# A graph network block on one core: the mixer's last multiply and add go from VectorE to GpSimd

## What is computed

```python
xn = _layernorm(x)
x = x + gnn(xn, ...) + mix(xn[None], ...)[0]
x = x + ffn(_layernorm(x), ...)

def mix(x, Wq, Wk, Wv, Wm, W1, W2, g1, b1, g2, b2):
    Q, K, v = elu(x @ Wq) + 1, elu(x @ Wk) + 1, (x @ Wv) / L
    KV = einsum('nshd,nshv->nhdv', K, v)
    Z = 1 / (einsum('nlhd,nhd->nlh', Q, K.sum(axis=1)) + eps)
    msg = (einsum('nlhd,nhdv,nlh->nlhv', Q, KV, Z) * L).reshape(N, L, C) @ Wm
    msg = _layernorm(msg, g1, b1)
    h = relu(concatenate([x, msg], -1) @ W1) @ W2
    return x + _layernorm(h, g2, b2)        # the change is in the "* g2" and in the sum

def gnn(...):                               # per edge: a score, a softmax per target, a weighted sum
    score = sum(q_att[etype, col] * k[row]) * pri[etype] / sqrt(64)
    agg = segment_sum(softmax(score) * v_msg[etype, row], col)
    return sigmoid(skip)[node_type] * typed_matmul(agg, a_linears, node_type)
```

## Time and profile before

| | |
|---|---|
| median of 3 runs | 2380.79 us (2377.87 to 2383.92) |
| span of the profiled execution | 2514.6 us (the page gives no time around it) |
| busy in the span | PE 2034.6, DVE 1762.5, ACT 1483.8, POOL 1180.2 us |
| mean granted clock of TensorE | 0.920 |
| DMA | 587 MB, 233 GB/s over the span |

### The profile page before, as it was taken

How to read it: one execution, slowest core, us unless ns; L and a number is a source line. 1 busy time by engine, 2 the same in 40 slices (tenths; PEclk the granted TensorE clock), 3 DMA queues, 4 the chain that set the end, 5 groups by cost and what they waited for, 6 DMA issues and landing times.

```text
span 2514.6 us, 38612 instructions
## 1 busy us (share of the span) xinstructions
PE 2034.6 (81%) x10630; PEld 1506.8 (60%) x10630; DVE 1762.5 (70%) x4682; ACT 1483.8 (59%) x4969; POOL 1180.2 (47%) x1207
## 2 busy tenths in 40 slices
PE   6999998985888888888888888888888774812999
PEld 5865554544666666666666666666666553611666
DVE  8867765544788888888888888888888664626121
ACT  6755554553667677777667676777767574620222
POOL 0033334335556565656655566556656413661231
PEclk9999999987999999999999999999999887965999
DMA  5868878986788887778878888888878837840110
GB/s 186 312 239 320 326 312 286 357 344 200 234 262 245 262 254 253 251 256 253 258 238 262 258 254 266 255 256 259 264 244 245 192 79 243 278 163 31 48 58 33
DMA packets 272145, 587.07 MB, mean 233 GB/s; under 512 B 45595, under 2 KB 186145, under 8 KB 265275
## 3 DMA queue, kind: packets, MB, share of 16 engines
q0 software_dynamic: 93936, 387.70, 47.1%
q1 hardware_dynamic: 177995, 196.89, 24.2%
HBM read 407.88 MB, written 176.99 MB: 233 GB/s over the span
## 4 chain that ended last, share of the span: by engine, by line
PE 46%; DVE 18%; ACT 14%; issue 10%; another core or an unknown queue 6%; DMA 4%; DVEq 1%; SPq 1%; POOL 0%; POOLq 0%; ACTq 0%
ACT arena L1267 10%; PE bank L904 7%; PE bank L739 7%; PE bank L872 4%; PE bank L893 4%; PE bank L1061 4%; PE bank L1072 4%; PE bank L718 3%; PE bank L587 2%; DMA arena<-chunk_rel 2%; DVE arena L1873 2%; DVE arena L1883 2%; PE bank L725 1%; DVE arena L1959 1%
## 5 line engine op out<-in xcount | busy, mean ns | idle before, releaser
L2248 POOL DMA_INDIRECT arena<-table,arena x880 | 862.9, 981 | 616.6 <-PE bank L904 360.7
L1267 ACT ACTIVATE arena<-arena 128x64 f32<-128x64 f32 x3520 | 857.3, 339 | 0.0
L904 PE MATMUL bank<-arena 128*128 128x260 f32 x1760 | 494.0, 420 | 58.7 <-issue 26.4
L904 PEld LDWEIGHTS bank<-arena 128*128 128x128 f32 x1760 | 342.9, 206 | 159.8 <-issue 65.3
L1873 DVE TENSOR_TENSOR arena<-bank,arena 128x512 f32<-128x512 f32 x440 | 300.3, 684 | 112.5 <-remote 52.5
L893 PE MATMUL bank<-arena 128*128 128x256 bf16 x2640 | 339.0, 279 | 11.5 <-issue 10.2
L893 PEld LDWEIGHTS bank<-arena 128*128 128x128 bf16 x2640 | 257.5, 100 | 73.4 <-issue 14.2
L1883 DVE TENSOR_REDUCE arena<-arena 128x16 f32<-128x1024 f32 x220 | 265.7, 1208 | 11.9 <-issue 0.5
L587 PE MATMUL bank<-arena 128*128 128x128 f32 (+1 forms) x643 | 127.2, 306 | 149.9 <-issue 47.6
L739 PE MATMUL bank<-arena 64*128 64x512 f32 x832 | 211.1, 624 | 22.3 <-DVE arena L1609 11.1
L872 PE MATMUL bank<-arena 128*128 128x256 f32 (+1 forms) x800 | 198.1, 393 | 7.5 <-issue 7.5
(11 more groups left out here) (310 smaller groups left out, 2978.2 us busy)
## 6 DMA issues: line engine op xcount, KB each, us to landing
arena<-q_parts SPq DMA_DIRECT2D x440, 192.0 KB
arena<-chunk_rel SPq DMA_DIRECT2D x220, 128.0 KB
arena<-table,arena POOLq DMA_INDIRECT x880
node_rows<-arena SPq DMA_DIRECT2D x24, 512.0 KB, 7.2
xl_and_sum<-arena SPq DMA_DIRECT2D x8, 1536.0 KB
arena<-in_x SPq DMA_DIRECT2D x12, 512.0 KB, 8.6
xn<-arena SPq DMA_DIRECT2D x12, 512.0 KB, 8.6
xT<-arena SPq DMA_DIRECT2D x12, 512.0 KB, 8.1
```

The costliest lines, as they stand in the source:

```text
L904: ins = TE.matmul(bank[b][:, 0:AW], lhsT=so[p % 2][:, c % 2, j, :], rhs=ring[:, c % NR, j, EX0:EX0 + AW], start=j == 0, stop=j == HALF - 1)
L1267: ins = A.activation(seg, seg, ACT.Copy, scale=rows[:, EX0 + h:EX0 + h + 1])
L2248: G.indirect_dma_start(ring[:, i % NR, j, :], None, d_tab_rows[0:N * R, :], bass.IndirectOffsetOnAxis(ap=idxE[:, g, j, c:c + 1], axis=0)). ...
```

## The change

DVE's two operations are taken out of its mixer, and with them the half step 10 of its table. POOL gets a function `add_base(g)` with the same multiply and the same add over the same buffers. It is called ahead of the gathers of pair 14, 23, 32 and so on (every ninth, 23 times inside the loop), and for the last two groups behind the last gather. A new semaphore, `base_scaled`, orders the add behind the multiply. All that waited for `mix_base` now waits for POOL's signal.

```diff
-DVE_AT = (2, 2, 4, 7, 10)
+DVE_AT = (2, 2, 4, 7)
+BASE_AT, BASE_PERIOD = 14, 9
...
         def mix():
             until = half_steps()
-            elu, y2s, ap, nrm, bas = DVE_AT
+            elu, y2s, ap, nrm = DVE_AT
...
-                if g:
-                    yield from until(g, bas)
-                    V.wait_ge(y2_normed, g)
-                    V.wait_ge(mbase_in.sem(g - 1), mbase_in.done(g - 1))
-                    into, part = base[:, 0:n_before, :], y2[:, 0:n_before, :]
-                    t = step(V.tensor_tensor(out=part, in0=part, in1=g2row.unsqueeze(1).to_broadcast([P, n_before, C]), op=ALU.mult))
-                    V.wait_ge(dve_step, t)
-                    V.tensor_tensor(out=into, in0=into, in1=part, op=ALU.add).then_inc(mix_base, 1)
...
+        def add_base(g):
+            n = len(mtiles(g))
+            into, part = base[:, 0:n, :], y2[:, 0:n, :]
+            G.wait_ge(mixw_in, 16 * 7)
+            G.wait_ge(y2_normed, g + 1)
+            G.wait_ge(mbase_in.sem(g), mbase_in.done(g))
+            G.tensor_tensor(out=part, in0=part, in1=g2row.unsqueeze(1).to_broadcast([P, n, C]), op=ALU.mult).then_inc(base_scaled, 1)
+            G.wait_ge(base_scaled, g + 1)
+            G.tensor_tensor(out=into, in0=into, in1=part, op=ALU.add).then_inc(mix_base, 1)
+
         for p in range(NPAIR):
+            if p >= BASE_AT and (p - BASE_AT) % BASE_PERIOD == 0 and (p - BASE_AT) // BASE_PERIOD < MG:
+                add_base((p - BASE_AT) // BASE_PERIOD)
             if p >= NR // 2:
...
+
+        for g in range((NPAIR - 1 - BASE_AT) // BASE_PERIOD + 1, MG):
+            add_base(g)
```

More of the change, by code:

```diff
@@ L499, in build @@
         sem("den_ready"), sem("averaged"), sem("averaged_too"), sem("rows_used"), sem("x1_stats"), sem("wa_scaled"), sem("slots_out"))
+    base_scaled = sem("base_scaled")
     cols_ready, inv2_built = sem("cols_ready"), sem("inv2_built")
```

## The result

On one chip, against the kernel before, the changed kernel took 2387.75 us in the median (2382.05 to 2399.23, 17 runs) and the kernel before 2380.0 us (2373.3 to 2394.98, 17 runs). The ratio is 1.0035, 95% interval 1.0021 to 1.005. So it is about 8 us slower. I had forecast 2378, 2.9 us faster.

The account below looks back on a forecast made before the run. It took hand-overs between in-order queues to bound the loop, with PE and DVE about equally full. -4.2 + 0 + 0.3 + 1 = -2.9 us on 2380.8 gave 2378 us; 8-in-10 range 2358 to 2392.

Parts of the forecast that it names:

- +1: GpSimd operand reads beside DVE's operations: they may keep each other out, costing 1 us in all.
- -4.2: DVE's multiply and add leaving its mixer: of 33.8 us freed, 4.2 us come off the time.
- late gathers: POOL's gathers behind each insertion: about 2.0 us late, covered by slack before the products, 0 us.
- my band of 2373.6 to 2387.9: Whole kernel's time: within 0.3% of the forecast 2378 us, given 50%.
- The four kinds of gaps: DVE after each L1847, by group number modulo 4: gaps absorb the 1.4 us; in kind 3 PE could use 0.3.
- The chain's three visits to L1847: Chain of work that ended last: passes DVE's base multiply in 3 groups of 25, 1.4 us each, 4.2 us.
- Rival (a): DVE in the loop sets the pace: gain 9.5 us (2371), or all 33.8 us (2347); chance 32%.
- Rival (b): GpSimd keeps out DVE operations with both inputs in SBUF, 2 x 1.35 us a group: 2390 to 2401; chance 13%.
- its deciding point of 1.4 us lost a group: DVE's loss to GpSimd in the mixer groups: it decides from 1.4 us lost per group.
- My margin of 9.6 us: POOL's gathers ahead of the products: 13.9 us from issue to use, 4.3 needed, leaving 9.6 us.
- The wait for normalised rows, the store, the tail (0, 0 and +0.3 us): Base rows ready 8 to 10 us early, store signal 11 us ahead, last group's base at most +0.3 us.
- sign (a): PE in the loop: its busy share rising by over 0.5% would show that DVE sets the pace.

Follow-up runs that it names:

- e1: The kernel before, unchanged, run once more for a profile on a 2380 chip: 2379.41 us.
- e16: Changed kernel with GpSimd's two operations replaced by a one-column memset that only signals, base left out, second run on a 2380 chip: ratio 0.9992.
- the memsets: Changed kernel with GpSimd's two operations replaced by five memsets that read nothing, base left out: ratios 1.0003, 1.0019, 1.0023 on 2380 chips, 1.0343 on a 2520 chip.
- the aligned version: Changed kernel with GpSimd's two operations ahead of an odd pair, waiting for DVE's edge targets: 2379.35 us, ratio 1.0015 (2380 chip); 1.036 (2520 chip).
- e17: Changed kernel with GpSimd's two operations replaced by three one-operand copies, base left out, on a 2380 chip: ratio 1.0013.
- e4: Kernel before, DVE keeping its base work, with GpSimd doing the same two operations on rows nobody reads: 2406.15 us, ratio 1.0124.
- e12: Changed kernel with GpSimd's two operations done twice at each place, the second time on dead rows, on a 2380 chip: 2405.81 us, ratio 1.0125.
- the signal: Changed kernel with GpSimd's two operations replaced by a one-column memset that signals, base left out, on 2380 chips: ratios 1.0003 and 0.9992.
- the copies: Changed kernel with three one-operand GpSimd copies in place of its two operations, base left out, on a 2380 chip: ratio 1.0013.
- the double dose: Changed kernel with GpSimd's two operations done twice at each place: 2405.81 us, ratio 1.0125 (2380 chip); 2636.2 us, 1.0471 (2520 chip).
- e2: Changed kernel with GpSimd's two operations replaced by five memsets that read nothing, base left out, on a 2380 chip: 2374.89 us, ratio 1.0003.
- e11, e13: A follow-up run on a 2380 chip; the text does not say under this number what it changed or measured.
- e15: Changed kernel with five memsets in place of GpSimd's two operations, base left out, on a further 2380 chip: ratio 1.0023.

## Why the prediction was wrong, point by point

- **The direction.** I forecast -2.9 us and measured about +8. The step that failed is "+1", what the two engines do to each other: I put it near the floor, and it cost about 8 us. "-4.2" and "0" for late gathers were each off by some 4 us besides, which their intervals hardly tell from nothing. The time of 2387.75 us lies just inside my band of 2373.6 to 2387.9, but only because the band reached into "slower": the ratio's interval lies wholly above 1, and the mechanism behind the forecast was not what happened.
- **The worth of DVE's 33.8 us (-4.2 us).** Right in kind, a little too large. With the two operations gone and nothing in their place the ratios are 1.0003 and 0.9992, -0.6 us in the mean, with intervals of 5 and 7 us to either side, so 4.2 is not excluded by them. The four kinds of gaps behind the earlier trace rows told it rightly: the time went into DVE's wait for PE ahead of the products, 53.3 us in e1 and 79.9 in e16, 27 of the 34 us. These are the groups of the two kernels:
```profile
L1873 DVE TENSOR_TENSOR arena<-bank,arena 128x512 f32<-128x512 f32 x440 | 300.8, 685 | 59.2 <-PE bank L893 53.3 <-DMA arena<-table,arena 5.4
```
```profile
L1867 DVE TENSOR_TENSOR arena<-bank,arena 128x512 f32<-128x512 f32 x440 | 300.4, 684 | 85.9 <-PE bank L895 79.9 <-DMA arena<-table,arena 5.5
```
 In the changed kernel the same wait is 58.4 us:
```profile
L1867 DVE TENSOR_TENSOR arena<-bank,arena 128x512 f32<-128x512 f32 x440 | 300.4, 684 | 64.0 <-PE bank L895 58.4 <-DMA arena<-table,arena 4.7
```
 So of the 29 us of hold-ups some 21 went into the wait that the freed time had become, which is why they cost less than they last. The chain's three visits to L1847 are a count of places where DVE came last, not of time that would be got back. Rival (a) did not hold on 2380 chips.
- **What the two engines do to each other (+1 us).** This is the step that failed. I put it "near the floor, as most DVE operations there read a bank of PSUM or one operand". Most do, but POOL meets DVE wherever its gathers let it, and at 14 of the 23 places in the loop the multiply started about 1.36 us ahead of L1924, with make_oh between. At every one of the 14 make_oh and GpSimd's own add were held up, and at 8 of them a third operation, L1941 or L1901, too. At four places (680.8, 910.35, 1368.14 and 1828.36 us) nothing was. DVE lost 29 us over 25 groups, 1.2 us a group, close to one GpSimd operation each. The price: the changed kernel's three ratios on 2380 chips have the mean 1.0048, the memsets' three 1.0015. The difference, 0.33% or 8 us (4 to 12 by the intervals), is what the hold-ups cost, and the aligned version (1.0015), where they are gone, stands where the memsets stand. Rival (b) was the right one. Its 2 x 1.35 us a group were twice what was lost, and its 2390 to 2401 us a little too high, for I measured 2387.75, and 2391 by the mean of the ratios; its deciding point of 1.4 us lost a group was too high as well, for 1.2 us already cost. The price does not grow in proportion: 17 us of hold-ups (e17) gave a ratio of 1.0013, 29 gave 1.0048, and 42 to 44 gave 1.0124 (e4, where DVE had kept its own work) and 1.0125 (e12, where GpSimd's time had doubled too). I gave it 13%, and the sum should have taken a price between the ends.
- **How long GpSimd takes.** I said 1.35 us for each operation and measured 1.28 for the multiply and 1.27 for an add that nobody holds up; most adds were held up and took 1.81. An insertion was to take 3.3 us and takes 3.13 in the mean of 23, from its first operation to the next gather. The last group's half-width pair took 0.73 and 0.72 us against my 0.7 each.
- **Late gathers (0 us).** On 2380 chips nearly right: the memsets' mean, 0.15% or 4 us, is all that is left for GpSimd's time, and none of the three intervals lies wholly above 1.0. On 2520 chips the loss is 60 us, and 80 with memsets. My margin of 9.6 us rested on 4.3 us from issue to use at the loop's start and on one place in the loop. That place was typical of the tightest (13.9 us from issue to use; the least is 13.3 in the changed kernel), so what I costed, rows that land too late for their product, is not what the trace shows to fail; another wait, which I had no term for, grew. I never asked what the 52.5 us of products waiting for "remote" were, in the same profile.
- **The wait for normalised rows, the store, the tail (0, 0 and +0.3 us).** Right: POOL waited for ACT once, 40.3 us, before the last group, where the gathers were over. GpSimd's last add ended at 1994.53, ahead of DVE's last addition at 1996.1, and SP's long waits for the base are two, as in the earlier trace rows:
```profile
SPq L2462 <- POOL arena L2241: 37.5, 2, 32.4
```
- **The base of the sum.** I carried us over from a span of 2514.6 to a time of 2380.8 as from "a slower execution". It was the 2520 kind, on which this very change costs five to seven times as much (ratio 1.0238 against 1.0048 and 1.0035).
- **What would show it.** I named longer L1930 and L1908 as signs of (b). The first was there, as the changed kernel's L1924 (up to 2377 ns). L1908, now L1902, stayed at 0.21 us; its neighbours L1901 and L1906 were the ones held up. PE's busy time in the stretch from 620 to 1940 us was 1150.2 us in e1 and 1143.7 in the changed kernel, so sign (a) was absent.

Not every us of DVE's is worth the same. The changed kernel has 4 us less of DVE's busy time than the kernel before, and is slower. My reading is that the base stood ahead of gaps that hid it, while the hold-ups fall on make_oh, the edge targets and the chain over rows, in front of work that PE takes up. This is argued, not shown: which of them carries the 8 us was not tried by itself. PE's wait at the end of the chain over rows, the likeliest place by the earlier trace rows, doesn't show it: 51.0 us in e1 and 52.4 in the changed kernel. A row that did grow is PE's wait for DVE's addition to `acc` before it can sum again, here in e1 and in the changed kernel (us, times, longest):
```profile
PE bank L904 <- DVE arena L1959: 12.8, 15, 6.6
```
```profile
PE bank L906 <- DVE arena L1953: 20.9, 22, 12.0
```
The other two profiles of the changed kernel on 2380 chips have 19.0 and 18.3 us, those of the signal and the memsets 3.3 to 14.1. But the copies, which cost nothing, have 17.4 and the double dose 13.4, so this row points to a place and settles nothing. It stays open.

## What to carry to other kernels

Moving work from VectorE to GpSimd frees VectorE only if GpSimd's reads of SBUF don't meet VectorE's operations with two operands in SBUF, or comparisons like make_oh; look at what VectorE runs at the instants when GpSimd is free. Holding GpSimd behind a signal of VectorE's took the hold-ups away here, but it gained nothing over the kernel before on a 2380 chip and cost 3.6% on a 2520 chip. Before costing the freed time, ask where VectorE waits next: here 27 of 34 us became a longer wait for PE. And the price of keeping an engine from its gathers differed here from chip to chip, so compare the span of a profile with the times before building on its margins.

## What the runs showed of the hardware

- A GpSimd operation of two 128x512 f32 operands takes 1.27 us, 1.9 times VectorE's 0.68. Held up by L1924 it took 1.81.
- VectorE's operation on 1x4 elements, 153 ns otherwise, took up to 1118 ns beside it. What a held-up operation takes goes by the GpSimd operation beside it and not by its own size.
- A copy on GpSimd (752 ns in the mean, one operand) holds VectorE up too. A memset hardly does: DVE busy 1731.6 to 1734.4 us against 1729.6 to 1730.6, of which make_oh has 2 to 4 us (80.0 to 80.9 against 77.0 and 77.7, its longest 846 ns). The reduction L1877, the additions L1953 and the products L1867, which have an operand in PSUM, never took longer beside GpSimd (at most 1224, 428 and 694 ns in the changed kernel, e2, e4, e11, e12, e13, e15 and e17; 1224, 426 and 693 in e1).
- Between chips the same kernel differs by 5.9% (2380 and 2520 us), with a granted clock of 0.931 and 0.920 and PE busy 2005.4 and 2034.6 us, and the same change costs 0.35 to 0.57% on one kind and 2.4% on the other. Whether the chip or something that lasted for a set makes the difference was not tried.
